# A two-layer cross-attention kernel on one core: item 0's own path first in every queue, the forms' Gram from VectorE's pairs, and new step orders

## The chip, the cores and the metric

The kernel runs on one core of one Trainium2 chip, in one launch. The metric is the device time of that launch in microseconds (us). Inputs come from and the output goes to the chip's memory; the arrays are prepared on the host before the launch.

## The reference, cut to what matters

Sixteen items are computed independently. Each has 256 rows of 256 values (x) and 77 rows of context. Layer L0 is self-attention, cross-attention to the context and a gated MLP, each behind an RMS norm; layer L1 attends from the result to the context, passes a rank-5 bottleneck, and attends within it.

```python
def attention(x, ctx, wq, wk, wv, wo):            # 16 heads of 16 values
    q, k, v = heads(x @ wq), heads(ctx @ wk), heads(ctx @ wv)
    attn = softmax(einsum('bqhd,bkhd->bhqk', q, k) * HD ** (-0.5))
    return merge(einsum('bhqk,bkhd->bqhd', attn, v)) @ wo

h = x + attention(rmsnorm(x, sa_norm_w), itself, sa_wq, sa_wk, sa_wv, sa_wo)
h = h + attention(rmsnorm(h, ca_norm_w), context, ca_wq, ca_wk, ca_wv, ca_wo)
h = h + (silu(rmsnorm(h, mlp_norm_w) @ w_gate) * (rmsnorm(h, mlp_norm_w) @ w_up)) @ w_down   # 1024 wide

norm_X, norm_F = layernorm(context), layernorm(h)
attended = softmax(norm_F @ norm_X.T / 16) @ norm_X
h4 = gelu(attended @ fc1_w.T + fc1_b)             # 4 values a row
cross = h4 @ fc2_w.T + fc2_b                      # so rank 5 with the bias
n = layernorm(cross)
out = norm_F + gamma2 * (cross + gamma1 * softmax(n @ n.T / 16) @ n)
```

## The kernel before

Every engine has its own queue of **steps**, and a step is a function called with the item's number n. `ORDER` lists each engine's steps of one period, with how many items ahead each is (`name@ahead`); `MOVED` shifts single steps of single items; `sequence(engine)` sorts all (step, item) pairs by their place. Steps of neighbouring items thus interleave. Engines wait for each other by semaphores inside the steps, and an engine goes through its queue strictly in order, so what stands ahead of a step in a queue delays it. In the following, `S.sa.0#1` is step `S.sa.0` of item 1.

The steps that matter here:

- `wl.k`, `ws.k`: weight k is loaded (SyncE) and split into a rounded high part (ScalarE) and the rest (VectorE). k runs over sa_wq, sa_wk, sa_wv, ca_wk, ca_wv, sa_wo, ca_wq, ca_wo, gate, up, down. Every product of weights is three passes over such parts (`product`, L1516). Weights 0 to 7 are staged in `probs`, gate and down in `late_a`, up in `late_b`.
- `norm.sa`, `ms.sa`, `xn.sa`, `T.sa`: squares and their sum (ScalarE, L1021), mean (VectorE), power -0.5 (GpSimd, L843), scaling (VectorE, L1254), the transposes on TensorE (L1524) and the split of what they give on ScalarE and VectorE (L1030, L1259).
- `qk.sa`: the q and k products (L1516), the split (L1067, L1279), then `pqk.sa.0` and `pqk.sa.1`, six DMAs that pack the parts for the score products (L779). `v.sa` are the value products.
- `S.sa.0` to `S.sa.7`: raw scores (L1589), of which VectorE takes the maximum (L1285); `maxsplit.sa` (L1295), `maxT.sa` (L1596) and the DMA `mr.sa` (L804) put the maxima into the packed q; `E.sa.0` to `E.sa.7`: shifted scores (L1609), their Exp on ScalarE (L1092), the products with v, `pv.sa.g` (L1623). The same for `ca` with half as many steps.
- `gT.g`, `gk.g`, `gv.g`, g from 0 to 4: the context of all items at once, 256 rows a group: transposed (L1535), its keys and values computed (L1516), and stored by `sk.g`, `sv.g`; `cl.g` loads the rows. They run once, beside items 0 and 1.
- `gu.m`, `hi.m`, `dnp.m`, m from 0 to 7: the MLP, 128 of 1024 inner columns at a time: gate and up products, Tanh (ScalarE, L1109) and two VectorE steps (L1338, L1340), split (L1119 and GpSimd, L847), down product (L1656). `T.mlp` are the transposes ahead of them.
- `nXT`, `nFT`, `sc`, `sce`, `pT`, `h4`, `xT`, `s2`, `mT2`, `e2`, `u2`, `fT`, `f2`, `out`: layer L1. `h4` on ScalarE is a Gelu (L1152), for which a set of activation tables is loaded; the next Exp loads another.
- `kt`, `kg`, `km`, `fold`, `fc`: once, constants of layer L1. `kt` turns the centred rows of fc2 (with its bias, 5 rows) and writes them as `wcT` and, scaled and with one row more, as `w6T`. `kg` (`gram`, L1706) makes 11 x 5 inner products of them over the 256 columns into one PSUM area: for each of 11 rows and each half of the columns a product whose left operand is one column broadcast to 128 x 128 and whose right operand has 5 columns.
- `IDLE`: before a step named there, TensorE does that many products of the identity with itself (L1488), which nothing reads.

The PSUM tile pair `ring` is passed on in the order of TensorE's queue: a step waits until the step that had its tile two places earlier has been read.

Of the kernel before, what the change touches and what calls it, by code (L numbers as in the profile page):

```python
# [72 lines left out]
        wo.sa@0 aT.ca@-1 S.sa.2@1 gT.1@2 dn@-2 s2@-3 wo.ca@-1 S.sa.3@1 ws.1@4 ms.mlp@-1 xn.mlp@-1 S.sa.4@1 ms.ca@0 ws.3@3 T.mlp@-1 gT.0@8 S.sa.5@1 fs@-3
        S.sa.6@1 xn.ca@0 gu.0@-1 S.sa.7@1 maxsplit.sa@1 gT.2@1 T.ca@0 u2@-3 lnstat.nf@-2 gu.1@-1 ws.7@1 ws.0@5 qk.ca@0 kg@0 lncen.nf@-2 gu.2@-1 gu.3@-1
        ms.sa@2 ws.4@3 lnstat.nx@-1 ws.8@1 S.ca.0@0 gk.3@0 gk.0@2 S.ca.1@0 sc@-2 xn.sa@2 ws.10@0 S.ca.2@0 S.ca.3@0 ws.5@2 maxsplit.ca@0 gk.1@1 T.sa@2 h4@-2
        o.sa.0@1 gu.4@-1 ws.6@2 ws.2@4 qk.sa@2 gT.4@0 gu.5@-1 out@-3 xs@-2 lncen.nx@-1 o.sa.1@1 hv@-2 oT.sa@1 gu.6@-1 aT.sa@1 km@4 gu.7@-1 o.ca.0@0 gT.3@1
# [26 lines left out]
def steps_of(engine):  # L103
# [282 lines left out]
def build(nc, x, ctx, w, vecs, norm_w, fc1t, fc1b, w5, out):  # L386
    st = ExitStack()
    with st:
# [3 lines left out]
        def sem(name):  # L392
            return st.enter_context(nc.semaphore(name))
# [1418 lines left out]
```

## Time and profile before

| | |
|---|---|
| median of 3 runs | 943.6 us |
| lowest, highest | 936.27, 945.41 us |
| the profiled execution | 944.47 us |
| its span | 942.7 us |
| its mean granted TensorE clock | 0.971 |

The span runs from the first to the last instruction of the profiled execution; 1.8 us of that execution lie around it. The profile's times are read against 944.47 us, and 944.47 lies 0.9 us above the median.

### The profile page before, as it was taken

The numbers are of one execution on the slowest core, as the hardware profiler recorded it, in microseconds if no ns is written. First come the engines' busy times: TensorE is split into PE (matmuls) and PEld (weight loads), VectorE is DVE, ScalarE is ACT, GpSimd is POOL, SyncE is SP. The second block draws the span as 40 slices with busy tenths as digits, with TensorE's granted clock in tenths as the row PEclk, the third lists the DMA queues.
The fourth block names the chain that finished last, engine by engine and source line by source line (L and its number), as shares of the span: only waits on it lengthen the run. The fifth ranks groups of instructions, "written<-read, shape, count | busy, mean of one in ns | idle before, by whom it ended". The sixth has DMA issues, their size and how long they took to land.

```text
span 942.7 us, 21297 instructions
## 1 busy us (share of the span) xinstructions
PE 882.9 (94%) x8154; PEld 750.2 (80%) x8154; DVE 667.6 (71%) x1443; ACT 546.2 (58%) x1098; POOL 253.2 (27%) x511
## 2 busy tenths in 40 slices
PE   6878889999999999999999999999999999979887
PEld 6766677787878888888888788888888887868786
DVE  4557576858596877778695968787786959565562
ACT  4445356474756566665747566666757474654543
POOL 7100011232231323332322223233323222242330
PEclk9899799999999999999999999999999999998997
DMA  6552422131131222222211312122222112111000
GB/s 206 191 180 94 134 75 81 44 105 42 54 104 43 93 65 80 78 80 60 99 37 57 101 53 90 57 81 78 80 77 81 42 59 83 44 33 35 16 13 22
DMA packets 74659, 71.73 MB, mean 76 GB/s; under 512 B 17632, under 2 KB 67408, under 8 KB 74560
## 3 DMA queue, kind: packets, MB, share of 16 engines
q1 hardware_dynamic: 74560, 70.39, 23.6%
q8 instruction: 65, 1.06, 0.5%
q14 instruction: 34, 0.28, 0.1%
HBM read 22.85 MB, written 9.24 MB: 34 GB/s over the span
## 4 chain that ended last, share of the span: by engine, by line
PE 77%; DVE 11%; ACT 6%; issue 3%; DMA 1%; POOL 1%; SPq 0%; ACTq 0%; DVEq 0%
PE mring L1516 21%; PE ring L1516 13%; PE down_ps L1656 9%; PE od L1623 9%; PE ring L1609 7%; PE ring L1589 6%; DVE mx_sa L1285 3%; PE ring L1524 2%; ACT probs L1092 1%; PE mring L1685 1%; PE mring L1761 1%; DVE late_a L1332 1%; PE od L1488 1%; PE ring L1596 1%; PE mring L1666 1%
## 5 line engine op out<-in xcount | busy, mean ns | idle before, releaser
L1092 ACT ACTIVATE probs<-ring 128x1024 f32<-128x1024 f32 (+1 forms) x192 | 190.9, 1022 | 46.8 <-PE ring L1609 43.0
L847 POOL TENSOR_TENSOR hidT_lo<-late_a,hidT_hi 128x256 fp32r<-128x256 f32 x128 | 95.8, 750 | 317.6 <-ACT hidT_hi L1119 316.4
L1285 DVE TENSOR_REDUCE mx_sa<-ring 128x4 f32<-128x1024 f32 x128 | 153.3, 1215 | 11.9 <-PE ring L1589 11.8
L1290 DVE TENSOR_REDUCE mx_ca<-ring 128x4 f32<-128x308 f32 x128 | 55.1, 474 | 61.4 <-PE ring L1589 61.1
L1338 DVE SCALAR_TENSOR_TENSOR late_a<-late_a,mring 128x256 f32<-128x256 f32 x128 | 52.9, 413 | 48.9 <-ACT late_a L1109 48.5
L1656 PE MATMUL down_ps<-down_hi,hidT_hi 128*128 128x256 f32 x256 | 79.1, 309 | 0.0
L1109 ACT ACTIVATE late_a<-mring 128x256 f32<-128x256 f32 x128 | 48.4, 378 | 50.9 <-PE mring L1516 48.8
L1589 PE MATMUL ring<-pk_sa 63*128 63x256 f32 x512 | 63.1, 330 | 11.4 <-DVE mx_sa L1285 5.3
L1656 PE MATMUL down_ps<-down_lo,hidT_hi 128*128 128x256 f32 x256 | 71.3, 279 | 0.0
L1656 PE MATMUL down_ps<-down_hi,hidT_lo 128*128 128x256 f32 x256 | 71.3, 278 | 0.0
L1119 ACT ACTIVATE hidT_hi<-late_a 128x256 fp32r<-128x256 f32 x128 | 52.6, 413 | 27.0 <-DVE late_a L1340 19.9
L1623 PE MATMUL od<-probs,vz_sa 128*32 128x256 f32 x1024 | 66.7, 388 | 0.7 <-ACT probs L1092 0.7
L1589 PEld LDWEIGHTS ring<-pk_sa 63*128 63x128 f32 x512 | 39.0, 188 | 33.1 <-issue 10.0
L1516 PE MATMUL mring<-hT_m_hi,gate_hi 128*128 128x256 f32 x256 | 60.2, 317 | 5.2 <-DVE hT_m_lo L1259 4.0
L1279 DVE TENSOR_TENSOR qkT<-ring,qkT 128x512 fp32r<-128x512 f32 x48 | 31.7, 687 | 42.1 <-ACT qkT L1067 42.1
L1609 PE MATMUL ring<-pk_sa 64*128 64x256 f32 x512 | 57.0, 319 | 1.7 <-ACT probs L1092 1.4
L1340 DVE SCALAR_TENSOR_TENSOR late_a<-late_a,mring 128x256 f32<-128x256 f32 x128 | 53.8, 421 | 4.4
L1303 DVE STREAM_TRANSPOSE late_b<-od 128x512 f32<-128x512 f32 x64 | 45.5, 710 | 14.2 <-PE od L1623 13.7
L1656 PEld LDWEIGHTS down_ps<-down_hi,hidT_hi 128*128 128x128 f32 x256 | 48.1, 188 | 9.2 <-issue 4.5
L843 POOL TENSOR_TENSOR mlp_rstd<-mlp_meansq,half_neg 128x2 f32<-128x2 f32 x16 | 11.2, 700 | 156.1 <-DVE mlp_meansq L1248 156.1
L1516 PEld LDWEIGHTS mring<-hT_m_hi,gate_hi 128*128 128x128 f32 x256 | 39.7, 194 | 16.1 <-DVE hT_m_lo L1259 5.1
L1516 PE MATMUL mring<-hT_m_lo,up_hi 128*128 128x256 f32 x256 | 52.2, 286 | 0.0
(334 smaller groups left out, 2329.6 us busy)
## 6 DMA issues: line engine op xcount, KB each, us to landing
pk_sa<-qkT SPq DMA_DIRECT2D x96, 256.0 KB, 2.8
qpk_ca<-qkT SPq DMA_DIRECT2D x48, 256.0 KB, 2.6
x_sb<-x SPq DMA_DIRECT2D x16, 256.0 KB, 2.9
x_res<-x SPq DMA_DIRECT2D x16, 256.0 KB, 3.0
out<-o_sb SPq DMA_DIRECT2D x16, 256.0 KB, 2.2
kpk_ca<-k_ca SPq DMA_DIRECT2D x48, 77.0 KB, 2.7
vz_ca<-v_ca SPq DMA_DIRECT2D x16, 154.0 KB
v_ca<-v_all SPq DMA_DIRECT2D x4, 512.0 KB, 3.4
```

The lines of the kernel that those rows point to most:

```text
L847: nc.gpsimd.tensor_tensor(hidT[1][:, m % HID, :], hid[:, m % 2, :], hidT[0][:, m % HID, :].bitcast(F32), ALU.subtract).then_inc(S["hidlo"] ...
L1092: nc.scalar.activation(granule(g, tag)[0:rows_, i0:i0 + 2, :, :].rearrange("p i h t -> p h i t"), ring_tile(("E", tag, k))[0:rows_].rearra ...
L1119: nc.scalar.activation(hidT[0][:, m % HID, :], hid[:, m % 2, :], ACT.Copy).then_inc(S["hidhi"].sem, 1)
L1285: nc.vector.tensor_reduce(mx[tag][:, :, :, k].rearrange("p q h -> p h q"), ps[:].rearrange("p h (q t) -> p h q t", t=T), AX_X, ALU.max).th ...
L1290: nc.vector.tensor_reduce(mx[tag][:, :, half, 2 * C * (k % 2) + k // 2:2 * C * (k % 2) + k // 2 + C + 1:C].rearrange("p q i -> p i q"), v, ...
L1338: nc.vector.scalar_tensor_tensor(out=hid[:, m % 2, :], in0=hid[:, m % 2, :], scalar=1.0, in1=ps[:, 0:T], op0=ALU.add, op1=ALU.mult).then_i ...
L1340: nc.vector.scalar_tensor_tensor(out=hid[:, m % 2, :], in0=hid[:, m % 2, :], scalar=0.5, in1=ps[:, T:2 * T], op0=ALU.mult, op1=ALU.mult).t ...
L1516: last = mm(outs, left(a, k % chunks), right(b, k % chunks), start=(k == 0), stop=(k == total - 1))
L1589: last = mm(ps[:, half, col:col + kw], qpk[tag][r, slot, q * P:(q + 1) * P], kpk[tag][r, slot, :], start=True, stop=True)
L1609: last = mm(ps[0:rows_, half, u * T:(u + 1) * T], kpk[tag][r, slot, kt * P:kt * P + rows_], qpk[tag][r, slot, :], start=True, stop=True)
L1623: last = mm(od[32 * i:32 * i + 32, half, :], vz[tag][0:rows_, kt, 8 * c + 2 * i + half, :], granule(g, tag)[0:rows_, i, half, :], start=(k ...
L1656: last = mm(down_ps[:, q, :], hidT[a][:, m % HID, q * P:(q + 1) * P], wt["down"][b][:, m, :], start=(m == 0 and q == 0 and k == 0), stop=( ...
```

## The change

Three things change.

1. In every queue item 0's way to its first scores stands first: on ScalarE `norm.sa#0` ahead of all weight splits, on GpSimd `ms.sa#0` behind the first of three groups of memsets, on VectorE `ms`, `xn`, `T` ahead of the splits of ca weights, on TensorE `T.sa#0`, `gT.0`, `qk.sa#0` ahead of `gk.0`, `gv.0`. On SyncE's queue the first two weights are issued ahead of `cl.0`, and both packs of item 0 ahead of `sv.0`, `sk.0`, `cl.2`.
2. The Gram: VectorE multiplies all pairs of rows elementwise (`row_pairs`, two instructions) and TensorE sums them over the partitions with one product of 55 columns for each half.
3. All tables (`ORDER`, `MOVED`, `IDLE`) are new. In items 3 to 14 ScalarE's Gelu `h4` of item n-3 now stands ahead of `E.sa.7` of item n. The numbers of idle products before steps of item 0 change, for one: 27 before `T.sa#0` and 8 before `qk.sa#0`, none before.

```diff
     "act": """
-        gu.3@-2 E.sa.2@0 E.sa.3@0 nFT@-3 gT.1@1 gT.4@-1 hi.2@-2 E.sa.4@0 fT@-4 ws.9@0 E.sa.5@0 E.sa.6@0 sce@-3 kg@1 T.sa@1 fc@1 pT@-3 gk.3@-1 maxT.ca@-1
+        gu.3@-2 E.sa.2@0 E.sa.3@0 nFT@-3 gT.2@0 E.sa.4@0 fT@-4 hi.2@-2 ws.3@4 E.sa.5@0 E.sa.6@0 sce@-3 T.sa@1 pT@-3 maxT.ca@-1 gu.4@-2 hi.3@-2 h4@-3 E.sa.7@0
...
 IDLE = {
-    ("gk.0", 0): 18, ("S.sa.7", 0): 4, ("maxT.sa", 0): 3, ("E.sa.0", 0): 11, ("S.sa.0", 1): 7, ("S.sa.7", 1): 5, ("E.sa.0", 1): 4,
-    ("E.sa.2", 1): 1, ("E.sa.7", 1): 2, ("e2", 13): 5, ("gu.0", 15): 5, ("nFT", 15): 7, ("fT", 14): 3, ("f2", 14): 12, ("s2", 15): 4,
-    ("mT2", 15): 3, ("e2", 15): 2,
+    ("T.sa", 0): 27, ("qk.sa", 0): 8, ("gk.0", 0): 17, ("S.sa.7", 0): 4, ("E.sa.0", 0): 12, ("E.sa.7", 0): 1, ("S.sa.0", 1): 9, ("T.ca", 0): 2,
+    ("E.sa.0", 1): 3, ("E.sa.3", 1): 4, ("S.ca.2", 0): 1, ("mT2", 13): 3, ("T.mlp", 15): 2, ("nFT", 15): 4, ("pT", 15): 5, ("fT", 14): 13,
+    ("mT2", 15): 4, ("fT", 15): 2,
 }
...
+            def row_pairs(n):
+
+                if at_first(n):
+                    dve.wait_ge(s_wc, 4)
+                    for a, rows, at0 in ((wcT, RANK, 0), (w6T, RANK + 1, RANK * RANK)):
+                        shape = [P, C, rows, RANK]
+                        dst = pairs[:, :, at0:at0 + rows * RANK].rearrange("p c (j k) -> p c j k", k=RANK)
+                        nc.vector.tensor_tensor(dst, a[:, :, 0:rows].unsqueeze(3).to_broadcast(shape), a[:, :, 0:RANK].unsqueeze(2).to_broadcast(shape), ALU.mult).then_inc(s_pairs, 1)
...
             def gram(n):
 
                 if at_first(n):
-                    pe.wait_ge(s_wc, 4)
-                    for row in range(FEAT + 1):
-                        src = wcT if row < RANK else w6T
-                        k = row if row < RANK else row - RANK
-                        for c in range(C):
-                            last = mm(down_ps[:, 1, row * RANK:(row + 1) * RANK], src[:, c, k:k + 1].to_broadcast([P, P]), src[:, c, 0:RANK],
-                                      start=(c == 0), stop=(c == C - 1))
+                    pe.wait_ge(s_pairs, 2)
+                    pe.wait_ge(s_vset, 3)
+                    for c in range(C):
+                        last = mm(down_ps[:, 1, 0:(FEAT + 1) * RANK], ones[:, 0:1].to_broadcast([P, P]), pairs[:, c, :], start=(c == 0), stop=(c == C - 1))
                     last.then_inc(s_gram, 1)
```

ScalarE's queue at the start of the program, before. `xn_a` is the scaled x, `hT_m` the turned context, `mring` its PSUM tiles:

```order
L1000 ACT_TABLE_LOAD
L1000 ACTIVATE sa_wq_hi<-probs,normw 128x256 x2
L1039 ACTIVATE hT_m_hi<-mring 128x512
L1000 ACTIVATE sa_wk_hi<-probs,normw 128x256 x2
L1000 ACTIVATE sa_wv_hi<-probs,normw 128x256 x2
L1003 ACTIVATE ca_wk_hi<-probs 128x512
L1021 ACTIVATE xn_a,sa_sumsq<-x_sb 128x256 x2
L1003 ACTIVATE ca_wv_hi<-probs 128x512
L1047 ACTIVATE hidT_hi<-mring 128x512
L1057 ACTIVATE v_all<-mring 128x32x16
L1030 ACTIVATE hT_a_hi<-ring 128x512
```

And of the change (its line numbers are 32 higher here):

```order
L1053 ACT_TABLE_LOAD
L1053 ACTIVATE xn_a,sa_sumsq<-x_sb 128x256 x2
L1032 ACTIVATE sa_wq_hi<-probs,normw 128x256 x2
L1032 ACTIVATE sa_wk_hi<-probs,normw 128x256 x2
L1062 ACTIVATE hT_a_hi<-ring 128x512
L1032 ACTIVATE sa_wv_hi<-probs,normw 128x256 x2
L1071 ACTIVATE hT_m_hi<-mring 128x512
L1035 ACTIVATE ca_wk_hi<-probs 128x512
L1099 ACTIVATE qkT<-ring 128x2x256 x2
```

The squares of x moved from behind five weight splits to the front, and the split of the turned x (`hT_a`) from behind the context's keys and values to behind two weight splits.

TensorE's queue around the Gram, before, with the last rows of item 0's k product ahead of it and the first scores behind it:

```order
L1516 MATMUL ring<-hT_a_lo,sa_wk_hi 128x256 x2
L1516 MATMUL ring<-hT_a_hi,sa_wk_lo 128x256 x2
L1706 MATMUL down_ps<-wcT 128x5 x10
L1706 MATMUL down_ps<-w6T 128x5 x12
L1589 MATMUL ring<-pk_sa 128x256 x8
```

And of the change, where the context's values and the turn of group 1 stand ahead of it:

```order
L1557 MATMUL mring<-ca_wv_lo,hT_m_hi 128x256 x2
L1557 MATMUL mring<-ca_wv_hi,hT_m_lo 128x256 x2
L1576 MATMUL mring<-ident,h_ca 128x128 x4
L1745 MATMUL down_ps<-pairs,ones 128x55 x2
L1630 MATMUL ring<-pk_sa 128x256 x8
```

The 22 products of 5 columns are two of 55, and the key and value products of group 0 moved from ahead of item 0's transposes to between its q, k products and its first scores.

ScalarE's queue in the middle of the program (item 8), before, from `maxT.ca` (`mT`) to the first Exp of the cross-attention (77 rows):

```order
L1082 ACTIVATE mT<-ring 16x256
L1092 ACTIVATE probs<-ring 128x2x2x256
L1119 ACTIVATE hidT_hi<-late_a 128x256
L1109 ACTIVATE late_a<-mring 128x256
L1152 ACT_TABLE_LOAD
L1152 ACTIVATE feat<-hpre 128x2x4
L1067 ACTIVATE qkT<-ring 128x2x256 x2
L1119 ACTIVATE hidT_hi<-late_a 128x256
L1109 ACTIVATE late_a<-mring 128x256
L1092 ACT_TABLE_LOAD
L1092 ACTIVATE probs<-ring 77x2x2x256 x2
```

And of the change:

```order
L1114 ACTIVATE mT<-ring 16x256
L1141 ACTIVATE late_a<-mring 128x256
L1151 ACTIVATE hidT_hi<-late_a 128x256
L1184 ACT_TABLE_LOAD
L1184 ACTIVATE feat<-hpre 128x2x4
L1124 ACT_TABLE_LOAD
L1124 ACTIVATE probs<-ring 128x2x2x256
L1099 ACTIVATE qkT<-ring 128x2x256 x2
L1151 ACTIVATE hidT_hi<-late_a 128x256
```

The last Exp of the self-attention (`E.sa.7`) moved from ahead of the Gelu to behind it, and with it the second table load; the number of loads is the same.

## Rows read from the trace of the kernel before

**Rows 1.** The profile's page, part 1, and one group of part 5.

```profile
PE 882.9 (94%) x8154; PEld 750.2 (80%) x8154; DVE 667.6 (71%) x1443; ACT 546.2 (58%) x1098; POOL 253.2 (27%) x511
...
L1285 DVE TENSOR_REDUCE mx_sa<-ring 128x4 f32<-128x1024 f32 x128 | 153.3, 1215 | 11.9 <-PE ring L1589 11.8
```

**Rows 2.** Busy us and instructions of each engine in stretches, with TensorE's granted clock and DMA.

```profile
30.00:40.00 10.00, 9.45 (x64) 8.07 (x62) 5.94 (x5) 3.52 (x5) 0.00 (x0) 0.76 0.98 322
...
500.00:600.00 100.00, 97.97 (x950) 83.37 (x948) 77.81 (x169) 62.59 (x128) 30.62 (x64) 1.00 0.22 68
```

**Rows 3.** TensorE's longest wait between 160 and 840 us: total, times, longest.

```profile
PE ring L1516 <- DVE mx_sa L1285: 7.0, 13, 0.5
```

**Rows 4.** The timeline, 0 to 17 us: start, duration, engine, operation, count, idle time before it.

```profile
5.42 1.09 PE L1535 MATMUL mring<-ident,h_ca 128*128 128x128 f32 x4 [5.42 <-DMA h_ca<-ctx]
...
6.30 6.41 PE L1488 MATMUL od<-ident 128*128 128x128 f32 x36
...
7.74 1.28 ACT L1000 ACT_TABLE_LOAD   x1 [7.74 <-DMA probs<-w_sa_wk]
...
11.17 0.87 DVE L1241 SCALAR_TENSOR_TENSOR sa_wq_lo<-probs,normw,sa_wq_hi 128x256 fp32r<-128x256 f32 x2
...
15.28 1.08 POOL L843 TENSOR_TENSOR sa_rstd<-sa_meansq,half_neg 128x2 f32<-128x2 f32 x1 [5.39 <-DVE sa_meansq L1248]
...
16.39 1.10 DVE L1254 TENSOR_SCALAR xn_a<-x_sb,sa_rstd 128x256 f32<-128x256 f32 x2 [0.61 <-POOL sa_rstd L843]
```

**Rows 5.** The chain of work that ended last, 0 to 54 us: start, duration, engine and line.

```profile
9.03 0.91 ACT sa_wq_hi L1000 x2
...
15.26 3.13 PE mring L1516 x24
...
20.28 3.14 PE ring L1516 x24
...
26.86 2.62 DMA pk_sa<-qkT
...
29.52 1.22 PE ring L1589 x8
30.75 2.86 PE mring L1516 x12
...
43.72 0.19 DVE nm_sa L1295
...
44.35 2.46 PE od L1488 x22
...
53.59 0.63 PE ring L1524 x4
```

**Rows 6.** Two stretches, columns as in rows 2.

```profile
28.00:30.00 2.00, 0.74 (x6) 0.66 (x8) 0.00 (x0) 1.09 (x4) 0.00 (x0) 0.51 1.02 352
93.00:103.00 10.00, 9.45 (x59) 7.03 (x60) 4.74 (x12) 4.40 (x6) 0.00 (x0) 0.50 0.10 25
```

**Rows 7.** The timeline, 23 to 29 us: the Gram's products and the q, k split.

```profile
23.24 2.29 PE L1706 MATMUL down_ps<-wcT 128*128 128x5 f32 x20
...
24.07 1.29 DVE L1279 TENSOR_TENSOR qkT<-ring,qkT 128x512 fp32r<-128x512 f32 x2 [0.42 <-ACT qkT L1067]
...
25.39 2.88 PE L1706 MATMUL down_ps<-w6T 128*128 128x5 f32 x24
```

**Rows 8.** The timeline, 460 to 465 us, on ScalarE, VectorE and TensorE.

```profile
460.11 1.03 ACT L1092 ACTIVATE probs<-ring 128x1024 f32<-128x1024 f32 x1 [0.41 <-PE ring L1609]
...
461.73 1.28 ACT L1152 ACT_TABLE_LOAD   x1
...
463.02 0.21 ACT L1152 ACTIVATE feat<-hpre 128x8 f32<-128x8 f32 x1
...
463.87 1.29 DVE L1279 TENSOR_TENSOR qkT<-ring,qkT 128x512 fp32r<-128x512 f32 x2 [1.26 <-ACT qkT L1067]
...
464.74 1.93 PE L1623 MATMUL od<-probs,vz_sa 128*32 128x256 f32 x32
```

**Rows 9.** The timeline of TensorE, 845 us.

```profile
845.34 0.77 PE L1516 MATMUL mring<-hT_m_hi,gate_hi 128*128 128x256 f32 x2 [1.50 <-DVE hT_m_lo L1259]
```

More of the change, by code:

```diff
@@ L71 @@
     """,
     "dve": """
[L73 to L76, printed above, removed]
@@ new lines @@
+    ("dve", "fc"): {0: 0.135802},
+    ("dve", "fs"): {14: 0.506173, 15: 0.444444},
+    ("dve", "gT.1"): {0: 0.518519},
+    ("dve", "gT.2"): {0: 0.222222},
+    ("dve", "gT.3"): {0: 0.160494},
+    ("dve", "gk.2"): {0: -0.065844},
+    ("dve", "gk.3"): {0: 0.306173},
+    ("dve", "gk.4"): {0: 0.117284},
+    ("dve", "gu.0"): {0: 0.08642, 14: 0.012346},
+    ("dve", "gu.1"): {14: -0.041152},
+    ("dve", "gu.2"): {14: -0.074074},
+    ("dve", "gu.5"): {9: -0.037037},
+    ("dve", "gu.6"): {14: 0.04321, 15: 0.176955},
@@ new lines @@
+    ("dve", "gu.7"): {11: 0.061728, 12: 0.018519, 14: 0.040123, 15: 0.168724},
+    ("dve", "hv"): {14: 0.098765},
+    ("dve", "km"): {0: -2.588477},
+    ("dve", "kt"): {0: 0.802469},
+    ("dve", "lncen.nf"): {13: -0.020576, 14: -0.185185},
+    ("dve", "lnstat.nf"): {13: -0.102881, 14: -0.191358},
+    ("dve", "lnstat.nx"): {13: -0.345679, 15: -0.160494},
+    ("dve", "ms.ca"): {3: -0.049383, 14: -0.030864},
+    ("dve", "ms.mlp"): {0: -0.012346, 2: -0.037037},
+    ("dve", "ms.sa"): {0: -6.864198, 15: -0.061728},
@@ new lines @@
+    ("dve", "o.ca.0"): {13: -0.063786, 14: -0.055556, 15: -0.089506},
+    ("dve", "o.ca.1"): {13: -0.082305},
+    ("dve", "o.sa.1"): {1: -0.009877},
+    ("dve", "oT.ca"): {13: -0.072016},
+    ("dve", "oT.sa"): {14: -0.004115},
+    ("dve", "out"): {12: -0.018519, 14: 0.234568},
+    ("dve", "qk.ca"): {15: -0.09465},
+    ("dve", "qk.sa"): {0: -4.967078, 2: 0.02963},
+    ("dve", "s2"): {2: -0.067901, 3: -0.080247, 11: 0.020576, 13: 0.033951},
+    ("dve", "sc"): {0: -0.037037, 1: 0.024691, 2: -0.024691, 3: -0.067901, 14: -0.117284},
@@ L306 @@
+    ("sp", "sk.3"): {0: -0.217949},
+    ("sp", "sk.4"): {0: -0.333333},
+    ("sp", "sv.0"): {0: 0.692308},
+    ("sp", "sv.2"): {0: 0.273504},
+    ("sp", "vl.ca"): {0: -0.141026},
+    ("sp", "wl.10"): {0: -1.},
+    ("sp", "wl.6"): {0: -0.811966},
+    ("sp", "wl.8"): {0: -0.897436},
+    ("sp", "wl.9"): {0: -0.394872},
 }
@@ L507, in build @@
         w6T = sb("w6T", [P, C, RANK + 1])
+        pairs = sb("pairs", [P, C, (FEAT + 1) * RANK])
         k_ca = nc.dram_tensor("k_ca", (2, P, C, B * SKV), F32, kind="Internal").ap()
```

244 lines of the change are left out of this document (109 added, 135 removed), and 159 rows, old and new, of the table MOVED.

## The prediction, made before the changed kernel was run

> **What bounds the kernel now.** Part 1 of the page comes first: TensorE is busy for 94% of the span, VectorE for 71% [rows 1]. An average over stages says little, so the windows come next. From 160 to 840 us they look like the one that stands there: TensorE busy 98 of 100 us at the full clock of 2.4 GHz [rows 2]. Its longest kind of wait in those 680 us is 7.0 us in sum, the value products `v.sa` for a maximum, 0.5 us an item [rows 3]. New orders have next to nothing to gain there, and all the room to lose. At the start it is otherwise: from 30 to 40 us VectorE does maxima for 5.9 of 10 us, and TensorE, nominally busy, has a clock of 0.76 [rows 2]. So the start is followed by the timeline and by the chain of work that ended last, where one reads what each step waited for [rows 4, 5]. Until 53 us the chain runs over weights, the context's products, x's transposes, q and k, packs, maxima and shifted scores of item 0. What the change does there moves all that follows, since item 1 and the rest hang on item 0's steps.
>
> **To item 0's q and k.** Before, ScalarE's first work waits for sa_wk until 7.7 us, then loads its table in 1.28 us; the squares of x come five splits later, and the scaling on VectorE ends at 17.5 us [rows 4]. Now the squares are first. x's landing isn't shown. The context's first group, issued third, had landed by 5.4 us, and sa_wk, issued fifth, by 7.7 us [rows 4]; x is issued first, a microsecond before the context, so I take 4.4, with 3.5 and 5.7 as ends. The table makes it 5.7, the two squares 6.6 (two passes of that size took 0.91 [rows 5]), the mean 6.9, the power with its 1.08 us 8.1, the scaling with 1.1 us 9.3 us. GpSimd's first memsets are over by 5.0 us, which hides them.
>
> TensorE has 27 idle products ahead of the transposes, 54 records. The 36 records from 6.3 us took 6.41 us, 0.178 each, and 22 later took 2.46 us, 0.11 each [rows 4, 5]. From 1.5 us on, when the identity is there, they end between 7.5 and 11.1 us. I take 10.2, nearer to the first, because it is the start of the program in both; so the idle products cost 0.9 us of the gain, and none to 1.8 at the ends. Then transposes 0.6, ScalarE 0.6, VectorE 0.7, and the low part of sa_wk, which now stands behind that on VectorE, 0.87: q and k start at about 13.0 instead of 20.28 us. They take 3.1, the split 0.6 + 1.3 until 18.0, and the packs can be issued 7.4 us earlier than at 25.4 us [rows 5, 7]. From issue to the last landing they took 4.1 us, so the data are there at 22.1; the gate weights, 1 MB, are still in flight then, which may add 1 to 2 us.
>
> **To item 0's first scores.** Here the change gives part back, because what stood ahead stands behind now. On VectorE, after the q, k split: the masks (0.9), sa_wv and ca_wk low parts (0.87 and 0.7), so `gk.0` starts at 20.4. `gk.0` and `gv.0` took 3.13 us together [rows 5], with `kt` between them 23.9; ScalarE copies the values (0.6), `gT.1` waits for that and takes 0.6, which is 25.1. The pairs on VectorE wait for ScalarE's `wcT` and `w6T`, written by 23, and are two small instructions (0.2 to 0.3 us each by the 0.3 us of other small ones, 1.1 at the most, which is what a 128 x 256 pair takes beside GpSimd), so ready by 24. The summing product is four records. Before, 44 records of 5 columns took 5.15 us [rows 7]; four take 0.5, or 0.9 if 55 columns in four passes cost like 128 do. The first scores start at 25.5 instead of 29.52 us: **4.0 us earlier**. The saving of 4.6 us in the Gram is not added: before, most of it lay beside the packs' flight, and TensorE still waited 1.3 us for them. What is late now is the group's products.
>
> **From there to the maxima.** Before, `S.sa.0` began at 29.52 and the last maximum ended at 43.72, 14.2 us for eight maxima of 1.22 us, 9.8 us [rows 1, 5]. The rest is TensorE: the clock fell to its level of 1.2 GHz in 28 to 30 us, after the 5-column products and the wait [rows 6], and `gk.1` took 2.86 us instead of half of 3.13 [rows 5]. With no such stretch ahead and 1.3 us less of the same in `gv.1` and the scores, 2.2 us go; VectorE then is the bound, so it can't be over 3.0, and it is 0 if the clock falls anyway. The last maximum is expected at 37.5, **6.2 us earlier** (4.0 to 7.0). What comes late next is VectorE: behind it gate and up low parts and `gk.1` now stand before `xn.sa#1`, which I have at 46.9; the transposes of item 1, before at 53.6 [rows 5], would want it at 47.4. It just fits.
>
> **The middle.** The Exp of `E.sa.7` stands behind the Gelu in 12 items. Before, it ran at 460.1. Now there come first a Tanh and a copy (0.8), a table load (1.28), the Gelu (0.2) and a second load (1.28); with its own 1.03 it ends at 464.3, 3.2 us later [rows 8]. The products that read it are the second half of those from 464.74 on, that is at 465.7: 1.4 us of cover. The q, k split, 463.9 before, is 1.1 us later, ends at 466.3, and its tile is wanted at about 467. In return the Exp of the cross-attention no longer waits for a load. Sum 0, with -2 to +4 us for the small swaps on all engines.
>
> Here the trace and a rule differ. The load of rows 8 began 0.02 us after the Tanh before it and the Gelu 0.01 us after the load, so a switch cost 1.28 us. The Trainium skill, page "ScalarE: Activation LUTs", section "What ACT_TABLE_LOAD costs", has the same 1283 ns for the load and adds about 1380 ns of drain to every switch, 2.66 us. By the row the sum above stands; by the page two switches in a row would cost 2.8 us more than the cover has.
>
> **The tail.** Before the products of item 14's MLP TensorE waits 1.5 us for the split [rows 9]; now `e2#12` and `T.ca#15` lie there, 1.0 us of work. VectorE's `lncen.nx#15` leaves the way of `dn#15`, 0.3 us. But 13 idle products ahead of `fT#14` and the transposes behind may cost 1 to 2 us where 12 stood. Sum -0.5, -3 to +3.
>
> **Sum.** 944.5 - 6.2 + 0 - 0.5 = 937.8 us for an execution like the profiled one, which lies 0.9 above the median shown: **937 us**, 0.7% below 943.6. About 1% is what a measurement of this kernel can tell from no change.
>
> **The rivals.** (a) *The clock holds later too.* After the start there are more stretches at 1.2 GHz, the longest from 93 to 103 us with TensorE busy 9.45 of 10 us [rows 6]; a stretch like that loses up to half its length. The new idle products in items 0 and 1 may save it. For it speaks that each stretch follows a thin one, against it that neither thin places nor total idle work change much. 937 - 5 = 932 us. (b) *The gain is eaten at once.* Idle products at 0.178 us each, packs against the gate load, and `xn.sa#1` behind two 2.4 us splits: each can take 1 to 3 us back. Then 942 us. (c) *Slower: `E.sa.7` is too late.* If the Gelu's input comes 1.4 us later than before in a typical item, the values' products wait on ScalarE, and TensorE with all that is queued behind `pv.sa.3`. Each microsecond over the cover costs 12 us in all; the change as a whole is slower from 0.55 us an item on. With 1.5 us, 937 + 18 = 955 us. (d) *The same by a full drain.* If two switches in a row cost 1.4 us more each, which no row shows, the Exp ends 2.8 us later, 1.4 past the cover, 12 times: 937 + 17 = 954 us. This is the rule of the page named above. (e) *The orders do nothing*, because the start isn't what the end hangs on: 943 us. The chain speaks against it, since it goes through item 0's steps without a break.
>
> **How the numbers follow.** The forecast has 0.46, its own range is 932 to 941; (a) 0.26, (b) 0.12, (c) 0.08, (d) 0.03, (e) 0.05. The range that leaves out no more than 2 in 10 reaches from (a) to beyond (b): 929 to 945. Faster by over 1% is below 934.2: most of (a) and a seventh of the forecast, 0.32. Slower by over 1% is above 953: most of (c) and (d) with wide steps, 0.09. Within 1%: 0.59.
>
> **What would show it.** The timeline: squares of x at 5.7, q and k at 13, first scores at 25.5, last maximum at 37.5 us, four records of the Gram, and a clock of 1.00 in the windows from 24 to 36 us. If first scores come at 25 and the span shrinks by less than 3 us, the loss has to be in the waits of items 0 and 1. In the middle the waits of TensorE on ScalarE's `probs` must stay near nothing; over 5 us of them in sum is rival (c) or (d), and the gap between the two loads tells which. The prediction is wrong if x lands after 6 us, if the middle's items are longer, or if the clock of the first 120 us is another.

## The result: 0.45% slower

| | before | changed |
|---|---|---|
| median | 943.25 us | 947.72 us |
| lowest, highest of 12 runs each | 936.27, 945.74 | 941.12, 950.87 |
| profiled execution, its span | 944.47, 942.7 | 947.8, 945.9 |
| mean granted TensorE clock | 0.971 | 0.984 |

The ratio is 1.0045, with a 95% interval of 1.0024 to 1.0067: a small loss where 937 us was forecast. The clock is the better one of the two, so the loss isn't there.

Part 1 of the page of the changed kernel, and its windows (columns as in rows 2), against [rows 1, 2, 6]:

```profile
PE 883.2 (93%) x8164; PEld 747.1 (79%) x8164; DVE 666.1 (70%) x1445; ACT 544.9 (58%) x1098; POOL 251.5 (27%) x511
```

```profile
30.00:40.00 10.00, 7.50 (x60) 6.09 (x60) 7.42 (x7) 3.33 (x6) 1.66 (x10) 1.00 0.64 224
500.00:600.00 100.00, 96.90 (x930) 81.74 (x923) 75.37 (x165) 61.52 (x126) 27.82 (x60) 1.00 0.20 63
93.00:103.00 10.00, 8.39 (x76) 6.52 (x75) 7.09 (x12) 3.56 (x6) 0.00 (x0) 0.83 0.16 56
```

From 30 to 40 us the clock is whole (0.76 before) and VectorE has more maxima in its 10 us. But from 500 to 600 us TensorE is busy for 96.9 us instead of 97.97 and runs 930 products instead of 950. An average hides how steady that is. A milestone shows it: one small instruction that each item has once, here VectorE's negated maxima of the cross-attention. The time from one to the next is called a period. In the timeline of VectorE these are items 3 and 12, in the kernel before,

```profile
251.39 0.18 DVE L1295 TENSOR_SCALAR nm_ca<-mx_ca 128x32 fp32r<-128x32 f32 x1
...
716.13 0.18 DVE L1295 TENSOR_SCALAR nm_ca<-mx_ca 128x32 fp32r<-128x32 f32 x1
```

and in the changed one:

```profile
247.34 0.18 DVE L1336 TENSOR_SCALAR nm_ca<-mx_ca 128x32 fp32r<-128x32 f32 x1
...
719.52 0.18 DVE L1336 TENSOR_SCALAR nm_ca<-mx_ca 128x32 fp32r<-128x32 f32 x1
```

Nine periods of (716.13 - 251.39) / 9 = 51.64 us became nine of 52.46. The change arrives 4.05 us early at item 3 and 3.39 late at item 12, each item costing 0.8. It is 5.92 late at item 14, wins 2.8 in the last period, and ends its span 3.2 us late: -4.05 at item 3, +7.44 over the nine periods, -0.2 from item 12 to the end.

The waits of TensorE from 160 to 840 us, changed kernel (total, times, longest), against [rows 3]:

```profile
PE ring L1557 <- DVE mx_sa L1326: 6.9, 13, 0.6
PE ring L1630 <- DVE mx_sa L1326: 5.8, 15, 0.6
PE ring L1630 <- DVE late_a L1373: 2.7, 8, 0.5
...
PE ring L1650 <- DVE qkT L1320: 1.6, 2, 1.2
```

The value products (L1557) wait as before. The raw scores (L1630) wait longer, in 15 places for maxima and in 8 for VectorE's part of `wo` (L1373). The cross-attention's scores (L1650) wait twice for the q, k split (L1320), 0.4 us in the period that ends at item 11 and 1.2 in that at item 13. Nothing is over 1.2 us: no single wait is the cause.

The start, as the chain of work that ended last, 0 to 54 us, changed kernel, against [rows 5]:

```profile
1.52 9.05 PE od L1529 x54
10.58 0.64 PE ring L1565 x4
...
13.51 3.12 PE ring L1557 x24
...
19.90 2.76 POOL sp L906
22.73 0.61 POOL o_sb L908
23.39 0.31 PE down_ps L1736 x2
23.70 1.64 PE mring L1557 x12
...
28.09 2.27 DVE mx_sa L1326 x2
...
40.05 0.19 DVE nm_sa L1336
...
50.04 0.63 PE ring L1565 x4
```

Two things are new. GpSimd stands on the chain, with 2.76 us for one multiplication of its `fold`, ahead of `kt` and of the value products of group 0. And VectorE's scaling of x, hidden here under the idle products, takes 3.61 us; its timeline with GpSimd's:

```profile
6.81 0.53 POOL L857 MEMSET vz_sa<- 128x512 f32 x1
6.90 3.61 DVE L1295 TENSOR_SCALAR xn_a<-x_sb,sa_rstd 128x256 f32<-128x256 f32 x2 [0.83 <-POOL sa_rstd L875]
7.27 1.81 POOL L858 MEMSET qpk_ca<- 128x2048 f32 x1
...
9.01 0.63 POOL L859 MEMSET kpk_ca<- 128x624 f32 x1
```

Before, the same scaling took 1.10 us [rows 4].

### The profile page after: what moved, and what is told of

The parts are those of the page before. It is cut to its first block, busy times and chain, and to the rows that moved or that the text cites. A ratio compares the mean times of both kernels' runs of the same rounds, so it can differ in the third digit from the quotient of the medians.

```text
span 945.9 us, 21319 instructions
## 1 busy us (share of the span) xinstructions
PE 883.2 (93%) x8164; PEld 747.1 (79%) x8164; DVE 666.1 (70%) x1445; ACT 544.9 (58%) x1098; POOL 251.5 (27%) x511
## 4 chain that ended last, share of the span: by engine, by line
PE 67%; DVE 18%; ACT 7%; issue 4%; POOL 1%; DMA 1%; SPq 0%; ACTq 0%; DVEq 0%; POOLq 0%
PE mring L1557 20%; PE ring L1557 9%; PE od L1664 7%; PE down_ps L1697 7%; PE ring L1650 7%; DVE mx_sa L1326 6%; PE ring L1630 5%; PE od L1529 2%; PE ring L1565 2%; DVE late_b L1344 1%; PE mring L1726 1%; DVE late_a L1373 1%; PE mring L1799 1%; DVE late_b L1352 1%; DVE late_b L1355 1%
## 5 line engine op out<-in xcount | busy, mean ns | idle before, releaser
L1379 DVE SCALAR_TENSOR_TENSOR late_a<-late_a,mring 128x256 f32<-128x256 f32 x128 | 52.3, 409 | 36.6 <-ACT late_a L1141 36.2
L1630 PE MATMUL ring<-pk_sa 63*128 63x256 f32 x512 | 61.6, 324 | 13.1 <-DVE mx_sa L1326 7.3
L1320 DVE TENSOR_TENSOR qkT<-ring,qkT 128x512 fp32r<-128x512 f32 x48 | 31.7, 687 | 56.2 <-ACT qkT L1099 52.4
L1557 PE MATMUL mring<-hT_m_hi,gate_hi 128*128 128x256 f32 x256 | 59.8, 315 | 6.6 <-DVE hT_m_lo L1300 3.2
L1630 PEld LDWEIGHTS ring<-pk_sa 63*128 63x128 f32 x512 | 38.2, 185 | 32.8 <-DVE mx_sa L1326 11.2
L1650 PE MATMUL ring<-pk_sa 64*128 64x256 f32 x512 | 57.2, 319 | 2.4 <-ACT probs L1124 1.1
L1557 PEld LDWEIGHTS mring<-hT_m_hi,gate_hi 128*128 128x128 f32 x256 | 39.2, 192 | 17.6 <-DVE late_a L1381 7.5
L1650 PEld LDWEIGHTS ring<-pk_sa 64*128 64x128 f32 x512 | 36.6, 185 | 20.7 <-DVE mx_ca L1331 5.1
```

Of the source, the lines that this page charges most:

```text
L1557: last = mm(outs, left(a, k % chunks), right(b, k % chunks), start=(k == 0), stop=(k == total - 1))
L1630: last = mm(ps[:, half, col:col + kw], qpk[tag][r, slot, q * P:(q + 1) * P], kpk[tag][r, slot, :], start=True, stop=True)
L1650: last = mm(ps[0:rows_, half, u * T:(u + 1) * T], kpk[tag][r, slot, kt * P:kt * P + rows_], qpk[tag][r, slot, :], start=True, stop=True)
```

## Experiments

Where two variants have the same orders, most of their periods agree within 0.05 us (an exception: the period that ends at item 8 is 52.71 in the changed kernel and 52.34 in e2, at the same orders). So for the middle one profiled execution of a variant tells more than many times do. The variants mix whole queues: `MIX` names for each engine from which kernel its queue is taken, up to an item's first score step (on ScalarE `maxT.sa`, on GpSimd `ms.sa`, on SyncE `mr.sa`). The idle products go with the head and with the tail.

### Head, middle and tail apart

```diff
-SEQUENCE = {e: sequence(e) for e in ORDER}
+MIX = every engine: [("after", 4), ("before", None)]                  # e1, new head
+MIX = every engine: [("before", 4), ("after", None)]                  # e2, old head
+MIX = every engine: [("after", 4), ("before", 13), ("after", None)]   # e3, old middle
+MIX = every engine: [("before", None)], the pairs on VectorE behind item 0's q, k split   # e4
```

> The queues of the changed kernel up to item 4's first scores on each engine, the old ones from there on (old idle products in the tail). Theory M (the new middle order costs 0.8 to 0.9 us an item in items 4 to 13, the head gives about 4 us): the negated maxima of item 3's cross-attention stay 4 us earlier than before, the periods after them are the old 51.6 us, the time is 939 (937 to 941). Rival P (the loss isn't in the order of the middle but in how the new head lets the items start, each period behind it is longer by 0.9 whatever the order): 947 us.

> The converse: the old queues up to item 4's first scores, the new ones from there on; the Gram is the new one. Theory M: head gain gone, middle loss kept, 4 us over the changed kernel, 951 us (949 to 953), periods 52.4 to 52.6 us. Rival P: old head, old periods, 943 minus the 2 to 3 us that the new tail gave, 941 us.

> New head to item 4, old queues for items 4 to 12, new tail from item 13's first scores on. Theory M: 9 us off the changed kernel, 938 (936 to 940); if the new tail is worth what the milestones say (item 15's period 41.7 against 44.5 us) this lies 2 to 3 us below the run with the new head alone. If the tail's gain was only the catching up of work left behind by the late middle, the two are equal. Rival P: 947.

> All old queues; only the Gram is the new one (two VectorE instructions behind the split of item 0's q and k, four TensorE records in place of 44). Theory: the first scores wait for the packs (29.5 us before), so nothing is gained there, 943 (942 to 944); TensorE waits 4 to 5 us instead of 1.3 ahead of them. Rival: the 5-column products had a cost behind them (the clock of 0.51 in the windows at 28 to 30 us), then up to 2 us less, 941; or the longer wait lowers the clock more, 944 to 945.

Start of the milestone in us, mean period, and the time from the last milestone to the end of the span, all of the profiled execution; the median is of 11 or 12 runs, and the ratio is to the kernel before, measured beside each (its median beside e1 to e4 was 943.0):

| | item 3 | item 12 | mean period | item 15 | to the end | median | ratio, 95% |
|---|---|---|---|---|---|---|---|
| before | 251.39 | 716.13 | 51.64 | 864.82 | 77.9 | 943.3 | |
| changed | 247.34 | 719.52 | 52.46 | 867.94 | 78.0 | 947.7 | 1.0045, 1.0024 to 1.0067 |
| e1, new head | 247.05 | 712.08 | 51.67 | 860.88 | 75.0 | 937.7 | 0.9954, 0.9929 to 0.9979 |
| e2, old head | 252.57 | 724.32 | 52.42 | 873.67 | 72.4 | 946.5 | 1.0043, 1.0022 to 1.0064 |
| e3, old middle | 248.44 | 713.68 | 51.69 | 862.14 | 78.1 | 941.4 | 0.9966, 0.9940 to 0.9991 |
| e4, Gram alone | 250.09 | 715.11 | 51.67 | 863.79 | 75.9 | 940.9 | 0.9965, 0.9943 to 0.9987 |

The mean period goes with the middle's orders (51.67 and 51.69 with the old ones, 52.42 with the new), whatever head stands ahead: theory M holds and P is out. The new head with the old rest is 0.46% under the kernel before. The new tail is worth nothing: in e3 it loses 2.5 us on e1 from item 12 to 14 and has them back at item 15, and the two ratios can't be told apart. For e2 I had 949 or more and got 946.5. Its profiled execution (947.8 us) is 4.8 us behind the changed kernel at item 12, as theory M says, and 5.7 at item 15, but its last stretch was 5.5 us shorter, with the same order. Windows of that stretch, first the changed kernel, then e2:

```profile
867.94:945.90 77.96, 63.87 (x479) 57.66 (x478) 35.58 (x111) 34.18 (x73) 21.87 (x40) 0.89 0.05 16
```

```profile
873.67:946.10 72.43, 58.09 (x479) 51.85 (x478) 35.59 (x111) 34.22 (x73) 21.93 (x40) 0.98 0.05 17
```

Same 479 products, a clock of 0.89 against 0.98, 5.5 us. So the clock of the tail can hide 5 us. The medians don't average it away either: that of e2 lies 1.2 us under that of the changed kernel, where the head should put it 4.8 over. What sets the tail's clock isn't shown.

The Gram alone gave 0.35%, 940.9 us, where I had expected 943; the rival with the clock behind the 5-column products had 941. The first scores still wait for the packs, and longer than before; e4's waits and window:

```profile
PE ring L1887 <- DMA pk_sa<-qkT: 4.6, 1, 4.6
```

```profile
30.00:40.00 10.00, 9.20 (x64) 7.85 (x64) 5.96 (x6) 3.73 (x5) 0.00 (x0) 0.83 0.98 329
```

The clock in that window is 0.83 (0.76 before), the last maximum is 0.2 us earlier, item 3 is 1.3 earlier. So some of it is clock in the first items. Part came ahead of the Gram: q and k started at 19.57 instead of 20.28 us in this profile. Whether these 1.3 us belong to the Gram or to where the clock happened to fall, one profile can't say; that there is a gain, the interval does.

### Which engine's order costs the middle's time

```diff
 MIX = every engine: [("after", None)], but
+"dve": [("after", 4), ("before", 13), ("after", None)]                # e5
+"act": [("after", 5), ("before", 13), ("after", None)]                # e6
+"pe":  [("after", 6), ("before", 13), ("after", None)]                # e7
+"sp" and "pool": [("after", 4), ("before", 13), ("after", None)]      # e8
+"pe" and "act":  [("after", 6), ("before", 13), ("after", None)]      # e9
```

> The changed kernel with VectorE's queue alone in the old order for items 4 to 12. Read from the milestone of each item (the negated maxima of its cross-attention), whose periods were 52.5 us changed and 51.65 us old, the same in several runs to 0.05 us. Theory V (VectorE's new order makes the score products wait for its maxima): periods of 51.7 to 52.0 us. Rival, TensorE's own new order makes the waits: 52.4 or more.

> The changed kernel with ScalarE's queue alone in the old order for items 5 to 12: the last Exp ahead of the Gelu again. If the prediction's rivals c or d held (E.sa.7 too late), periods fall by 0.5 us or more to 52.0; theory V or the rival of TensorE's order: they stay within 0.15 of 52.5.

> The changed kernel with TensorE's queue alone in the old order for items 6 to 12. If TensorE's order is the cause, periods of 51.7 to 52.0 from item 7 on; theory V: 52.3 or more, and perhaps worse, since VectorE's new order was made for the other one.

> The changed kernel with SyncE's and GpSimd's queues in the old order for items 4 to 12. Both theories: no change, periods within 0.1 of 52.5. If later loads or GpSimd's second splits are what is waited for: 52.0 or less.

> The changed kernel with TensorE's and ScalarE's queues in the old order for items 6 to 12. TensorE's alone gave periods of 52.2 between its two seams (52.6 changed, 51.7 old, means over items 7 to 11), ScalarE's alone took 0.13 to 0.25 off where nothing clashed. If those two parts add up, 51.9 to 52.0, and VectorE's new order costs the last 0.2 to 0.3; if VectorE's order is neutral, 51.7; if the three orders only fit as a set, more than 52.2.

Periods that end at items 7 to 11. An asterisk marks one over 54 us, where the old queue of one engine and the new ones of the others don't fit in some item; in both at item 11 TensorE's clock fell for some 4 us as well. They are left out of what follows:

| | 7 | 8 | 9 | 10 | 11 |
|---|---|---|---|---|---|
| before | 51.72 | 51.77 | 51.39 | 51.77 | 51.57 |
| changed | 52.45 | 52.71 | 52.52 | 52.23 | 53.15 |
| e5, VectorE old | 52.44 | 52.53 | 52.34 | 52.18 | 55.27* |
| e6, ScalarE old | 52.21 | 52.47 | 54.44* | 51.98 | 57.87* |
| e7, TensorE old | 51.91 | 52.37 | 51.55 | 52.32 | 52.71 |
| e8, SyncE and GpSimd old | 52.45 | 52.32 | 52.53 | 52.22 | 53.13 |
| e9, TensorE and ScalarE old | 51.91 | 51.95 | 51.55 | 51.98 | 52.38 |

The mean of these five is 51.64 before and 52.61 changed. TensorE's order takes 0.44 of the 0.97 back (52.17, where I had 51.7 to 52.0), ScalarE's another 0.22 (51.95, as the sum of the two parts said). The other 0.31 stays with the other three or with how the mixed queues fit, which these runs don't part. With e2's mean as the base (52.53, the same middle) TensorE's share is 0.36 of 0.89. SyncE's and GpSimd's order gave 0.08 (52.53) and VectorE's 0.10 (items 7 to 10), nearly all of it in item 8's period, where e2 has the same 52.3 with all orders new. So neither alone is worth anything that these periods show, and theory V fell. As whole kernels these five took 946.7 to 956.7 us (one time each): e8 and e9 lie within the changed kernel's runs (941 to 951), the others above them.

### The moved Exp, and the spacing of the scores

e10 and e11 move one step in ScalarE's order, e12 two in TensorE's:

```diff
-maxT.ca@-1 gu.4@-2 hi.3@-2 h4@-3 E.sa.7@0            # changed kernel
+maxT.ca@-1 E.sa.7@0 gu.4@-2 hi.3@-2 h4@-3            # e10
-ws.6@1 E.sa.7@0 hi.3@-2 gu.4@-2 ws.2@4 gv.2@0 h4@-3 qk.sa@1      # e1
+ws.6@1 hi.3@-2 gu.4@-2 ws.2@4 gv.2@0 h4@-3 E.sa.7@0 qk.sa@1      # e11
-wo.sa@0 dnp.5@-2 S.sa.2@1 ... wo.ca@-1 S.sa.3@1 ... nXT@-2 mT2@-3 S.sa.4@1      # e1
+wo.sa@0 S.sa.2@1 dnp.5@-2 ... wo.ca@-1 ... nXT@-2 mT2@-3 S.sa.3@1 S.sa.4@1      # e12
```

> The changed kernel with one step moved in ScalarE's order: the last Exp of the self-attention ahead of the Gelu (and of the Tanh and the split) again. Theory S (the loss sits in TensorE's order of score steps, ScalarE's share is 0.2 us an item): periods 52.3 to 52.5. Rivals c and d of the prediction: 52.0 or less. The two table loads must part: the Gelu then stands between two loads with the q, k split behind it.

> The converse: new head, all old orders from item 4 on (the run of the new head, 937.7 us, periods 51.65), with that one Exp behind the Gelu in every item. Theory S: periods 51.7 to 51.9 (the cover of 1.4 us holds). Rivals c and d: 52.1 or more, time 942 and up; in rival d the Exp would start over 2 us after the Gelu.

> New head, all old orders from item 4 on, with two moves in TensorE's order of the middle alone: the third score step ahead of a down product, and the fourth behind nXT and mT2, right ahead of the fifth, as in most items of the change. Theory S (the maxima take VectorE 1.2 us each and each score step waits for the one two places back, so unequal spacing makes waits): periods up by 0.2 to 0.5 us to 51.9 to 52.2, the waits of score products for the maxima (0.3 us an item) grow by as much. Rival (spacing doesn't matter, what counts is VectorE's other work): within 0.1 of 51.65.

In e11 the periods that end at items 7, 10 and 11 are 51.73, 51.78 and 51.85, against 51.73, 51.78 and 51.57 in e1. In e10 the early one gives 52.45 at item 7 and 52.26 at item 10, where the changed kernel has 52.45 and 52.23: the late Exp is covered in a typical item. It isn't in two: the early one takes the period that ends at item 11 from 53.15 to 52.84 and that at item 13 from 53.49 to 52.82, and the late one puts 0.3 and 0.4 us on the same two in e11. There it is the q, k split behind the Exp that comes late. TensorE's waits for it, 0.4 and 1.2 us in the changed kernel, are nothing and 0.5 in e10. That is 1 us of the 10 lost from item 3 to item 14.

But e10 has one period of 54.98 us, at item 9, and e11 has 55.15 and 53.33, so their whole times (945.1 and 947.5) say nothing of the Exp. In e10's long one TensorE waits 3.1 us in all, against 1.3 in the changed kernel; the longest, 0.8 us, is for VectorE's MLP step (L1340 in the kernel before), as it is in e6's long period at item 9. The rest of these 2.5 us wasn't followed.

e12 cost 0.5 us in six of the nine periods from item 3 to 12 (for instance 52.09 against 51.57 at item 11), 0.1 or nothing in two, and 1.5 in one, item 8, where the clock fell as well (to 0.50, 483 to 486 us). The waits between items 3 and 12, first e1, then e12:

```profile
PE ring L1814 <- DVE mx_sa L1583: 4.9, 9, 0.5
PE ring L1887 <- DVE mx_sa L1583: 2.9, 9, 0.5
```

```profile
PE ring L1814 <- DVE mx_sa L1583: 9.6, 9, 1.1
PE ring L1887 <- DVE mx_sa L1583: 2.6, 8, 0.5
```

L1814 is the value products, behind `S.sa.4`, and L1887 the score products; the expectation had put the growth on the latter. With two score steps back to back they wait 1.1 us an item for VectorE instead of 0.5, for a maximum takes about 1.2 us. So spacing has a price, 0.5 us an item. But the expectation's "as in most items of the change" holds for the earlier third step alone: `S.sa.3` stands right ahead of `S.sa.4` in 4 of the items 3 to 14 (3, 6, 7 and 8). And in the changed kernel this wait stayed at 0.5 an item (6.9 us in 13, against 7.0 in [rows 3]). So e12 shows what a swap can cost, not what cost the changed kernel its 0.8 us.

### The start again

```diff
 # e13: in e1's queues of item 0
+"pe":  kt behind S.sa.1, kg behind S.sa.6
+"act": kt behind ws.8
+"dve": kt behind S.sa.4
 # e14: e1 with
+                if at_first(n) and k == 1:
+                    pool.wait_ge(S["sa", "xn"].sem, S["sa", "xn"].at(0, QT))
-    ("T.sa", 0): 27
+    ("T.sa", 0): 18
 # e15: both
```

> The run of the new head (old orders from item 4 on, 937.7 us) with the centred rows, the pairs and the Gram behind item 0's first scores: on TensorE kt behind S.sa.1 and kg behind S.sa.6, on ScalarE kt behind the gate's split, on VectorE the pairs behind S.sa.4, in a gap of 1.1 us between two maxima. Theory F (the values of group 0 wait for GpSimd's fold by way of kt): gv.0 starts at 22.4 instead of 23.6, first scores at 25.6 instead of 27.05, last maximum 38.6 to 39.0 instead of 40.1, time 1 to 1.5 us less. Rival (packs or the context's splits are as late): scores at 26.7 or later, no change.

> The run of the new head with GpSimd's second group of memsets waiting until x is scaled, and 18 idle products ahead of item 0's transposes in place of 27. Theory D (the scaling on VectorE took 3.6 us instead of 1.1 because it ran beside these memsets): the scaling takes 1.1 us and ends at 8.0, transposes at 8.1 instead of 10.6, q and k at 11.2 instead of 13.5. Rival (the scaling is slow for another reason, such as the first use of its operands or the DMA traffic): still 3 us or more. What of it reaches the first scores is less, because the fold, the masks and the context's products stand ahead: 1 to 2 us, time 936 to 938.

> Both edits together. If the two hold and nothing else stands in the way, first scores at 23.5 to 24.5 (27.05 with the new head, 29.5 before) and the last maximum at 36.5 to 37.5, which is where the prediction had it (25.5 and 37.5); time 934 to 936. If the packs bound it (six issues of 4.6 us and 2 us of flight), first scores at 25 and little over the run with kt later. The start has idle TensorE time of its own, so the clock may fall elsewhere and take up to 2 us back.

The median of the kernel before is here that of the 11 runs beside e13 to e15; e1's line is from its own round. The times to item 3 are those of the profiled executions.

| | q, k start | first scores | last maximum | item 3 | median | ratio, 95% |
|---|---|---|---|---|---|---|
| before | 20.28 | 29.52 | 43.72 | 251.39 | 943.7 | |
| e1 | 13.53 | 27.07 | 40.09 | 247.05 | 937.7 | 0.9954, 0.9929 to 0.9979 |
| e13 | 13.56 | 25.49 | 39.34 | 246.32 | 935.6 | 0.9926, 0.9901 to 0.9952 |
| e14 | 10.68 | 24.23 | 37.23 | 242.27 | 936.5 | 0.9919, 0.9894 to 0.9945 |
| e15 | 10.46 | 22.38 | 36.24 | 244.76 | 935.3 | 0.9913, 0.9887 to 0.9939 |

The timeline of e14:

```profile
7.06 0.61 DVE L1553 TENSOR_SCALAR xn_a<-x_sb,sa_rstd 128x256 f32<-128x256 f32 x2 [0.83 <-POOL sa_rstd L1133]
...
7.74 0.53 POOL L1115 MEMSET vz_sa<- 128x512 f32 x1 [0.71 <-DVE xn_a L1553]
...
8.20 1.81 POOL L1116 MEMSET qpk_ca<- 128x2048 f32 x1
```

With the memsets behind it the scaling takes 0.61 us, less than the 1.1 that I had. Theory D is shown, and F with it: group 0's values no longer wait for the fold, and in e13 start at 22.55 instead of 23.65 us. That is 1.1 of the 1.6 us at the first scores; the other 0.5 is the summing product, which no longer stands ahead of them. The packs don't bind even at 22.4 us. Of the milestones, e13's last maximum is later than expected (38.6 to 39.0), and e14 and e15 have earlier first scores than expected. Of e15's 4.7 us at the first scores 3.9 are left at the last maximum and 2.3 at item 3. Its clock from 40 to 60 us is 0.74, that of e14 1.00:

```profile
40.00:60.00 20.00, 15.86 (x135) 11.14 (x133) 8.80 (x14) 10.01 (x13) 1.66 (x1) 0.74 0.32 107
```

```profile
40.00:60.00 20.00, 15.88 (x164) 11.86 (x164) 12.06 (x20) 10.63 (x15) 1.66 (x1) 1.00 0.45 146
```

All of e13 to e15 beat both kernels; the intervals don't tell them apart from each other or from e1.

## Why the prediction was wrong

**The step that failed is the middle**: "Sum 0, with -2 to +4 us for the small swaps on all engines". The new orders of the middle cost 0.82 us an item, 7.4 us over nine items and 10.0 from item 3 to item 14; with the old orders there (e1, e3) the loss is gone. That "the middle's items are longer" is one of the prediction's own signs of being wrong. The premise was read rightly ("next to nothing to gain there, and all the room to lose") and not used: I looked for one wait to take the place of another, checked the moved Exp, and priced all other swaps as noise around nothing, without a row for any of them. In a middle where TensorE is idle for 17 us in 680, a swap can win little and lose much. Ten items as a window, first before, then changed:

```profile
251.39:767.55 516.16, 504.22 (x4860) 428.49 (x4860) 397.09 (x860) 326.11 (x661) 151.98 (x320) 1.00 0.23 72
```

```profile
247.34:773.01 525.67, 508.61 (x4862) 429.73 (x4862) 393.30 (x861) 324.94 (x661) 147.89 (x319) 1.00 0.23 71
```

TensorE's idle time grew from 11.9 to 17.1 us, which are the small waits above, and its busy time from 504.2 to 508.6 with the same products. The single products overlap in the trace, and the sum of their durations is nearly the same in the two windows (749.8 and 751.9 us), so in the main they start further apart. What spaces them isn't shown, nor is which of the swaps cost how much: of the 0.97 us in items 7 to 11 the runs give 0.44 to TensorE's order and 0.22 to ScalarE's.

**Rivals (c) and (d)**, value products that wait for the Exp behind the Gelu, didn't come; what the moved Exp did cost is 1 us, by way of the q, k split in two items (e10). The changed kernel, ScalarE and then TensorE, against [rows 8]:

```profile
459.54 1.28 ACT L1184 ACT_TABLE_LOAD   x1
460.83 0.21 ACT L1184 ACTIVATE feat<-hpre 128x8 f32<-128x8 f32 x1
461.06 1.28 ACT L1124 ACT_TABLE_LOAD   x1
462.35 1.02 ACT L1124 ACTIVATE probs<-ring 128x1024 f32<-128x1024 f32 x1
```

```profile
463.99 1.93 PE L1664 MATMUL od<-probs,vz_sa 128*32 128x256 f32 x32
```

The Exp ends at 463.4, the products that read it come in the second half of 463.99 to 465.9, and TensorE's waits for `probs` sum to 0.2 us in the 680. Two switches in a row cost 1.29 and 1.29 us, with the Gelu's 0.21 us between them. The Trainium skill's page "ScalarE: Activation LUTs", section "What ACT_TABLE_LOAD costs", has 2.66 us for each with its drain; by that, an estimate, the Exp would have started 2.7 us later. The trace has no drain here. (The prediction's "2.8 us more than the cover has" is a slip: 2.8 is the whole of the two drains, 1.4 more than the cover, as its rival (d) has it.)

**To q and k: nearly right, and partly by luck.** q and k started at 13.5 (13.0). The idle products, which the forecast went by, ended at 10.6 (10.2 taken). Under them an error was hidden: x had landed at 3.6 us (4.4 taken), and still the scaling ended at 10.5 instead of 9.3, just in time. The sentence "GpSimd's first memsets are over by 5.0 us, which hides them" looked at the first group and not at the second, behind the power.

**To the first scores: 27.05 instead of 25.5.** I had `kt` "between" the context's products at no cost and listed VectorE's masks without following who waits for them: GpSimd's fold, whose second instruction took 2.76 us (0.87 before), then `kt`, then `gv.0`. The change was worth 2.5 us here, not 4.0; e13 moves `kt` and the Gram away and gives 1.6 back. That what is late is "the group's products" was right. The pairs (ready at 25.4, 24 taken) and the summing product (0.55 us, 0.5 to 0.9 taken) held nothing up. (The old Gram's 5.15 us is 5.17 by [rows 7]; nothing hangs on it.)

**To the last maximum: 40.05 instead of 37.5**, outside its range of 4.0 to 7.0 us by 0.3. 1.2 us of the 2.2 for the maxima came, with the clock at 1.00 as expected.

**The tail** came out as forecast (-0.5) in size: item 12 to the end of the span took 226.4 us, 226.6 before. There is luck in that: it is a loss of 2.5 us to item 14 and a gain of 2.8 in the period behind it, and e2, with the same order, had a last stretch 5.5 us shorter. **Rival (a)**, the clock: it did hold better, 0.83 from 93 to 103 us instead of 0.50. The self-attention's maxima of item 2 were 8.7 us early; those of item 3 were 4.9, since the time between them was 3.8 longer. e1 has the same, so it lies in the new head; why isn't shown. **Rival (b)**, a gain eaten at once, came in part: 2.2 of the 6.2 us were missing at item 3. **Rival (e)** is out: the new head alone gives 0.46% (e1).

## What to carry to other kernels

Where the bounding engine has no idle time, a new order is to be priced as a loss until each swap is shown free. The period of one milestone per item shows in one profile a loss in the middle that the clock of the start or the tail can hide in the medians of twelve runs. Take a large reordering apart by stretches before reading its waits: here a good head was sold with a bad middle. When a step is moved ahead on one engine, look at what the others do at the new time; at both places where the move brought VectorE and GpSimd together one of the two took 2 to 3 us longer.

## What the runs showed of the hardware

**VectorE and GpSimd.** A scaling of 128 x 256, twice, took 3.61 us beside memsets and 0.61 with them moved away (e14); a GpSimd product of two tensors took 2.76 us beside VectorE's weight splits, and 0.87 before (also in e2 and e4; no run moved this pair alone). The Trainium skill, page "SBUF — State Buffer", section "Who interferes with whom", says that the two share a port pair that one holds for a whole instruction, and that a `tensor_scalar` in a two-port mode and a VectorE instruction with two SBUF inputs (against a GpSimd one that reads) are among those that contend. Both cases fit in kind, but the wait was longer than one instruction: one of the two scalings took 3.35 us, where the longest memset beside it took 1.81, and the pair ended at 10.5 us, 0.4 behind the last of four memsets in a row. The GpSimd product ended at 22.6, behind VectorE's splits, which followed each other from 19.4 to 22.1. Whether the scaling ran in a two-port mode no row says.

**A hole in the middle can cost twice.** In seven of the variants (e5 to e9, e11, e12) TensorE's clock fell to its level of 1.2 GHz once or twice between 160 and 830 us, where neither kernel has it. e12, 214 to 223 us, and e7:

```profile
214.00:217.00 3.00, 3.00 (x28) 3.00 (x27) 2.87 (x5) 0.45 (x1) 0.00 (x0) 1.00 0.00 0
217.00:220.00 3.00, 1.47 (x14) 0.97 (x13) 2.40 (x4) 2.54 (x9) 0.09 (x1) 0.99 0.37 113
220.00:223.00 3.00, 3.00 (x15) 3.00 (x16) 1.82 (x4) 1.20 (x5) 1.06 (x2) 0.50 0.01 3
```

```profile
378.00:381.00 3.00, 1.32 (x12) 1.12 (x10) 2.26 (x4) 0.00 (x0) 0.00 (x0) 1.00 0.00 0
384.00:390.00 6.00, 6.00 (x29) 5.00 (x29) 3.83 (x7) 2.83 (x11) 0.70 (x1) 0.50 0.05 16
```

Before these two the engine was busy for half of 3 us or less; behind the first come 15 products in 3 us instead of 28. But a hole alone doesn't decide it. In e5 the engine was busy for 0.75 of 3 us, and the clock stayed at 1.00:

```profile
328.00:331.00 3.00, 0.75 (x8) 0.60 (x6) 2.99 (x4) 0.00 (x0) 0.00 (x0) 1.00 0.08 26
331.00:337.00 6.00, 4.89 (x39) 4.36 (x40) 3.19 (x6) 3.23 (x12) 0.70 (x1) 1.00 0.01 3
```

And in e11, with no such hole in sight (4.6 of 5 us busy just ahead), it fell too:

```profile
495.00:500.00 5.00, 4.60 (x49) 3.39 (x50) 1.92 (x8) 4.51 (x8) 1.17 (x3) 1.00 0.50 161
500.00:505.00 5.00, 5.00 (x52) 3.52 (x54) 2.69 (x9) 2.32 (x4) 1.23 (x2) 0.77 0.00 0
505.00:510.00 5.00, 5.00 (x33) 4.62 (x31) 1.91 (x5) 1.46 (x3) 0.00 (x0) 0.50 0.00 0
```

The low stretch lasts to 512 us and lies in its two long periods, 55.15 and 53.33 us. Why the clock fell there, and not in e5, stays open.
